# Moving the rotation of the next queries and the query product inside the steps of an attention

## The reference

```
q = (x @ Wq.T).reshape(b, s, 16, 128); k, v likewise with 4 heads
q = q * cos + rotate_half(q) * sin;    k = k * cos + rotate_half(k) * sin
scores = q k^T * 128**-0.5, masked;    attn = softmax(scores)
out = (attn v) reshaped to (b, s, 2048) @ Wo.T
```

## Time and profile before

| | |
|---|---|
| three runs | 840.57, 841.95, 836.37 us |
| the profiled execution: its time | 835.15 us |
| its span | 833.3 us |
| mean granted TensorE clock | 0.936 |
| PE busy | 712.8 us (86%) |
| DVE busy | 627.9 us (75%) |
| ACT busy | 458.0 us (55%) |
| POOL busy | 402.5 us (48%) |

### The profile page before, as it was taken

One profiled execution on the slowest core, in us unless ns is written; L12 is line 12 of the kernel. 1 busy time (PEld: TensorE's weight loads), 2 busy tenths in 40 slices (PEclk: granted clock), 3 DMA queues, 4 the chain that ended last, 5 costly groups with the idle time before them and its releaser, 6 DMA issues. The chain is left out here.

```text
span 833.3 us, 17601 instructions
## 1 busy us (share of the span) xinstructions
PE 712.8 (86%) x5515; PEld 481.6 (58%) x5515; DVE 627.9 (75%) x1436; ACT 458.0 (55%) x1033; POOL 402.5 (48%) x412
## 2 busy tenths in 40 slices
PE   7898969999969999989898699765698498978985
PEld 3555447777637777655555466433586397645652
DVE  5989878778787878699977677544897687676656
ACT  3444568878758888545423266325474476324551
POOL 4544766667667667358636177324004320331440
PEclk9999979999999999999999799966799598998998
DMA  9999995000000000030001233300000010012324
GB/s 375 327 300 185 226 231 2 0 0 0 2 0 1 0 0 0 6 116 1 1 14 58 77 114 110 129 1 1 1 1 2 7 46 2 1 52 84 116 84 164
DMA packets 64945, 59.07 MB, mean 71 GB/s; under 512 B 29106, under 2 KB 59186, under 8 KB 64370
## 3 DMA queue, kind: packets, MB, share of 16 engines
q1 hardware_dynamic: 60706, 47.85, 23.7%
q0 software_dynamic: 3744, 10.26, 3.5%
q10 hardware_dynamic: 432, 0.15, 0.1%
HBM read 27.92 MB, written 30.33 MB: 70 GB/s over the span
## 5 line engine op out<-in xcount | busy, mean ns | idle before, releaser
L1492 PE MATMUL PS<-XT,WA 128*128 128x512 f16 x432 | 100.4, 380 | 0.0
L607 POOL TENSOR_TENSOR ARENA<-ARENA,ST 128x512 f32<-128x512 f32 x64 | 66.6, 1040 | 64.0 <-DVE ST L1278 64.0
L724 ACT ACTIVATE ARENA<-T 128x512 f16<-128x512 f32 (+1 forms) x56 | 35.2, 628 | 109.9 <-DVE T L1156 102.4
L1492 PE MATMUL PS<-WA,ARENA 128*128 128x256 f16 (+2 forms) x960 | 68.6, 212 | 12.9 <-DVE ARENA L1165 11.9
L1492 PEld LDWEIGHTS PS<-WA,ARENA 128*128 128x128 f16 x960 | 56.6, 97 | 29.4 <-DVE ARENA L1165 18.0
L566 POOL DMA_INDIRECT yt_rows<-WA,DIX x46 | 45.4, 987 | 55.4 <-ACT WA L856 43.4
L1492 PEld LDWEIGHTS PS<-XT,WA 128*128 128x128 f16 (+1 forms) x432 | 42.3, 98 | 44.1 <-issue 0.8
L1492 PE MATMUL PS<-KVR,ARENA 128*128 (+1 forms) x384 | 57.9, 279 | 7.9 <-DVE ARENA L1250 4.6
L1258 DVE TENSOR_REDUCE ST<-PS 128x2 f32<-128x512 f32 x64 | 43.9, 686 | 26.1 <-PE PS L1492 25.3
L757 ACT ACTIVATE ARENA<-PS,ST 128x256 f32<-128x256 f32 x128 | 59.3, 470 | 7.0 <-DVE ST L1261 6.8
L1492 PE MATMUL PS<-XT,WC 128*128 128x512 f16 x264 | 60.6, 379 | 2.4 <-DVE T L1149 1.4
(11 more groups left out here) (184 smaller groups left out, 1803.0 us busy)
## 6 DMA issues: line engine op xcount, KB each, us to landing
xs_rows<-ROUT SPq DMA_DIRECT2D x2, 9252.0 KB, 46.1
WA<-xs_rows SPq DMA_DIRECT2D x46, 129.0 KB
WB<-wb_dram SPq DMA_DIRECT2D x1, 4096.0 KB, 21.4
WC<-wc_dram SPq DMA_DIRECT2D x1, 2304.0 KB, 26.5
WA<-wa_dram SPq DMA_DIRECT2D x4, 512.0 KB, 6.8
WA<-wa_dram SPq DMA_DIRECT2D x1, 2048.0 KB, 12.7
WA<-yt_rows SPq DMA_DIRECT2D x4, 512.0 KB, 4.1
WB<-yt_rows SPq DMA_DIRECT2D x4, 512.0 KB, 5.8
```

The costliest lines, as they stand in the source:

```text
L607: pl.tensor_tensor(pr, pr, rs.broadcast_to([P, 2, S]), ALU.mult).then_inc(norm_done, 1)
L724: sc.activation(HH[r, a, 0, :], T3[r, :], ACT.Copy).then_inc(hid_hi, 1)
L1492: ins = te.matmul(dst, left(a), right(b), start=first and n == 0, stop=last and n == 2, skip_group_check=True)
```

## The change

In `step0` of the first attention, each engine's part of a head's rotation and the query product are put at another place of the same instruction stream. POOL's `rope_sine` goes ahead of the normalising in odd steps. ACT's `rope_swapped` goes to the start of odd steps. DVE's `rope_cosine` goes from behind the row maximum of an even step to the end of the odd step before it. PE's query product goes from the end of its step to right behind the scores. No instruction and no wait is added or taken away.

```diff
--- before.py
+++ after.py
@@ -601,12 +601,12 @@
                     rope_add(r + 1, 1)
                 if x == 2 and more:
                     rope_add(r + 2, 0)
+                if x % 2 and more:
+                    rope_sine(r + 2 + x // 2, x // 2)
                 pool.wait_ge(recip_done, st + 1)
                 pr = PR0[:, x % 2, :].rearrange("p (q k) -> p q k", q=2)
                 rs = ST[:, x % 2, 3, :].rearrange("p (q k) -> p q k", k=1)
                 pl.tensor_tensor(pr, pr, rs.broadcast_to([P, 2, S]), ALU.mult).then_inc(norm_done, 1)
-                if x % 2 and more:
-                    rope_sine(r + 2 + x // 2, x // 2)
 
             def attention0(hf, n, th):
                 for i in range(KV0 + 2):
@@ -744,6 +744,8 @@
             def step0(hf, p, x):
                 st, r = NS0 * hf + 4 * p + x, RU * hf + KV0 + 2 * p
                 more, before = not (isinstance(p, int) and p >= P0 - 1), not (isinstance(p, int) and p in (0, P0))
+                if x % 2 and more:
+                    rope_swapped(r + 2 + x // 2, QB, x // 2)
                 if lagged(p, x, 2, P0):
                     act.wait_ge(pt_done, st - 1)
                     after(act, pv_done, st - 3)
@@ -761,9 +763,6 @@
 
                     act.wait_ge(pv_done, st - 2)
                     sc.activation(OT0[:, 1 - x % 2, 0, :], PS[:, OB, 0:S], ACT.Copy, scale=1 / SP).then_inc(ot_hi, 1)
-                if x % 2 and more:
-                    rope_swapped(r + 2 + x // 2, QB, x // 2)
-
                 if x == 0 and before:
                     act.wait_ge(scores, st)
                     rope_high(r + 1, 1, QT0[:, 1, 0, :])
@@ -1260,10 +1259,6 @@
                     dve.wait_ge(max_done, st + 1)
                     v.tensor_scalar(ST[:, x % 2, 1, :], ST[:, x % 2, 0, :], -SC0 / SQ ** 2, None,
                                     ALU.mult).then_inc(shift_done, 1)
-                if x == 0 and before:
-                    rope_cosine(r + 1, QB, 1)
-                if x == 2 and more:
-                    rope_cosine(r + 2, QB, 0)
                 if x == 1 and before:
                     rope_low(r + 1, 1, QT0[:, 1, 1, :], QT0[:, 1, 0, :])
                 if x == 3 and more:
@@ -1280,6 +1275,8 @@
                     dve.wait_ge(ot_hi, st - 2)
                     v.scalar_tensor_tensor(OT0[:, 1 - x % 2, 1, :], PS[:, OB, 0:S], 1 / SP, OT0[:, 1 - x % 2, 0, :],
                                            ALU.mult, ALU.subtract).then_inc(ot_lo, 1)
+                if x % 2 and more:
+                    rope_cosine(r + 2 + x // 2, QB, x // 2)
 
             def attention0(hf, n, th):
                 r = RU * hf
@@ -1686,6 +1683,8 @@
                             te.matmul(PS[:, bank, P:S], IDB[:, :], MASK[:, :], start=False, stop=True,
                                       skip_group_check=True)
                     ins.then_inc(scores, 1)
+                if x in ((1, 2) if isinstance(p, int) and p == 0 else (0, 2)) and not (isinstance(p, int) and p >= P0 - 1):
+                    queries(hf, 2 * p + 2 + x // 2, QB, r + 2 + x // 2, r + 2 + x // 2)
                 if lagged(p, x, 2, P0):
                     pe.wait_ge(norm_done, st - 1)
                     after(pe, pt_lo, st - 3)
@@ -1712,8 +1711,6 @@
                                       lambda s: WB16[:, 2 * pp + xx // 2, s, D:2 * D], False, False)
                     ins.then_inc(proj_done, 1)
 
-                if x in ((1, 2) if isinstance(p, int) and p == 0 else (0, 2)) and not (isinstance(p, int) and p >= P0 - 1):
-                    queries(hf, 2 * p + 2 + x // 2, QB, r + 2 + x // 2, r + 2 + x // 2)
 
             def attention0(hf, n, th):
                 r = RU * hf
```

## The result

The changed kernel takes 887.82 us in the median of four runs (883.76 to 890.63), the kernel before 839.45 (836.37 to 841.95). The ratio is 1.057, with a 95% interval of 1.051 to 1.064. The forecast was 888 us, with a range of 876 to 899.

The account below looks back on a forecast made before the run. PE was taken to bound the pair at 6.66 us; a ring of 8.62 us adds 47.0 over 24 pairs plus 2.6 at the starts, +49.6 us, giving 884.8 or 890.2. The forecast was 888 us, range 876 to 899.

Parts of the forecast that it names:

- What bounds the pair: First attention's loop, before: PE bounds a pair of steps, 6.22 us of work and 0.44 of waits in 6.66.
- The ring: First attention's loop: waits through PE, ACT and DVE close once per pair, summing to 8.62 us, 1.96 more than 6.66.
- the step from the output copy to `rope_high`: On ACT in the even step: 0.40 us from the output copy's start, then `rope_high` for 0.63.
- the transposes to the copy: From the start of PE's transposes to the start of ACT's copy that waits for them: 0.64 us.
- The term for the output's low part: On DVE in the odd step: 0.34 us until the cosine product starts; by the skill's rule 0.42, ring 8.70.
- How often: First attention: 24 pairs at 1.96 us make 47.0, plus 2.6 at the starts of both halves, +49.6 us.
- the one turn at the start of each half: One more ring turn at each half's start, costing 0 to 1.96 us; taken as 1.3, 2.6 for both.
- from the last query product to the last reciprocal of a half: End of each half: the last pair has no query product and stays as it is, 0 us.
- The parts at no cost: POOL's sine product has 3.1 us to spare; DVE's row maximum releases exponentials that wait for ACT's copy anyway: no cost.
- The delay did close into a ring: Rival, no ring: only the even step's transposes come later, 0.8 us in 24 pairs, 19 us, 854; 5%.
- The faster case: Rival: PE never waits ahead of the query product, 0.21 us per pair goes, 5 us, 830 or 834; 2%.
- The clock rival: Rival: PE's waits drop its clock to 1.2 GHz, a pair's PE work is 12.4 us, some 978; 3%.

Follow-up runs that it names:

- e12_cos_early_red: Changed kernel with DVE's cosine product moved behind `rope_low` of the odd step and the row maximum's scaling written as TENSOR_REDUCE; 840.34 us, 0.996 of before.
- e13_T_red: As e12_cos_early_red, with PE's query product moved between the transposes and the value product; 833.97 us, 0.987 of before.
- e1: Changed kernel with only DVE's cosine product moved behind `rope_low` of the odd step, ahead of the reciprocal and the output's low part; 856.17 us, 1.014 of before.
- e3: Kernel before with only PE's query product moved right behind the scores; 896.67 us, 1.059 of before.
- e4: Changed kernel with only POOL's sine product put back behind the normalising; 896.81 us, 1.063 of before.
- e14: Changed kernel with the scaling of the row maximum written as TENSOR_REDUCE; 894.07 us, 1.059 of before.
- e8: Changed kernel with only DVE's cosine product put back behind the row maximum of the next even step; 938.62 us, 1.111 of before.
- e2_query_back: Changed kernel with only PE's query product put back at the end of its step, behind the projection; 862.91 us, 1.023 of before.
- e5_T_scalar: As e13_T_red, but with the scaling in its old form, TENSOR_SCALAR; 855.61 us, 1.013 of before.
- e16_query_back_red: As e2_query_back, with the scaling written as TENSOR_REDUCE; 859.96 us, 1.017 of before.

## Why the prediction was right

**What bounds the pair.** Right: e12_cos_early_red and e13_T_red show that with no ring a pair goes to 6.6 and 6.4 us, PE's own work plus small waits.

**The ring.** Right in mechanism and place. Its sum was forecast at 8.62 us and measured 8.50 and 8.58. The term that was off is the step from the output copy to `rope_high`: I took 0.40 us, the distance to the swapped copies in the earlier trace rows, and it is 0.26 (158.43 to 158.69), in front of 0.67 for `rope_high` in place of its length of 0.63. The others held within 0.02, except for the transposes to the copy, 0.63 and 0.72 for a forecast 0.64. e1 (one edge of the ring out), e3 (a ring of its own from one move), e4 and e14 (not on the ring) and e8 (a longer ring) bear it out.

The term for the output's low part, 0.34 by the row, came out as 0.34 (162.41 to 162.75) and not 0.42. The section of the Trainium skill that the prediction set against it (page "VectorE: DVE Perf Modes", "The DRAIN you can't avoid") also says that a next operation that is not held starts earlier, which the prediction left out.

**How often.** The total of 49.6 us met the 49.7 measured in the attention by luck: three of its parts were off and made up for one another. From one query product to the next, start to start, the trace gives:

| | forecast | measured |
|---|---|---|
| the 24 pairs | +47.0 us | +46.0 us |
| the one turn at the start of each half, both together | +2.6 us | -2.0 us |
| from the last query product to the last reciprocal of a half, both together | 0 | +5.6 us |

The 46.0 hold 1.8 us of one pair of 10.27 us in the first half, where the clock was at its low level; its query product took 2.74 us in place of 1.47:

```profile
127.75 2.74 PE L1489 MATMUL PS<-XT,WB 128*128 128x512 f16 x6 [1.36 <-DVE T L1243]
...
138.02 1.47 PE L1489 MATMUL PS<-XT,WB 128*128 128x512 f16 x6 [1.42 <-DVE T L1243]
```

The turn at a half's start was forecast 1.3 us longer and became shorter, from 5.97 and 6.09 us to 5.17 and 4.94. The end of a half was said to stay and became 2.8 us longer, 18.6 in place of 15.75. The prediction counted query products and passed over their move inside the step: the transposes, the value product and the projection of the step, 1.75 us of PE work by the earlier trace rows, stood ahead of the last query product and now stand behind it. Most of the remaining 1.1 us at an end are longer waits of PE for DVE. At the end of the first half they are 0.81 and 1.14 us for the output's low part (at 231.28 and 235.03); before they were 0.42 for it and 0.55 for `rope_low` (at 207.24 and 209.26).

**The parts at no cost.** POOL's sine product cost nothing that shows: undoing its move made nothing faster (e4). That the cosine product's neighbours on DVE cost nothing held for the changed kernel only because ACT was late for another reason. The same change puts POOL's sum beside DVE's scaling, which took 0.74 us in even steps of the changed kernel where it took 0.17. I had named the POOL instructions as harmless by their readers alone, and not looked at which DVE instructions they run beside.

**The rivals.** The delay did close into a ring. The faster case was far off for this order. It came in e13_T_red, which keeps only the moves on ACT and POOL, has the cosine product and the query product at other places than the change, and the scaling in another form. The clock rival was right in kind and small here: one stretch of 8 us. In e8_cos_back, where PE waited 2.7 us in each pair in place of 1.7 to 1.9, it came again and again. The page "TensorE: Matmul & The Clock Gate" of the Trainium skill, section "A second HAM failure mode: psum-queue depth-cycling", which the prediction cites, is thus borne out in e8_cos_back (clock 0.74 and 0.91) and not in the changed kernel from 138 us to the end of its loop (1.00).

## What to carry to other kernels

Before an instruction is moved ahead of others on its engine, follow its wait round: who frees it, what that one waits for, and whether the chain comes back to what is now queued behind. The sum of that chain is the period, however idle each engine looks; here 8.5 us with no engine over 80% busy in these pairs. When such a move loses, the cure may be a few places elsewhere in the chain: with the instruction that frees the bank moved earlier, three quarters of the loss were gone. The rest took a look at what the moved instructions now run beside; with the scaling in another form the time was that of the kernel before, and with the query product behind the transposes 1.3% under it.

## What the runs showed of the hardware

- A DVE TENSOR_SCALAR of 128x2, SBUF to SBUF, that comes while POOL works on its 128x512 TENSOR_TENSOR doesn't finish before POOL's has: 1.21, 1.14 and 0.74 us in place of 0.17, each end within 0.04 us of POOL's (after, e1_cos_early, e2_query_back, e5_T_scalar). As a TENSOR_REDUCE with the same output it is 0.16 us beside the same POOL instruction (e12_cos_early_red, e14_after_red). The Trainium skill, page "SBUF — State Buffer", section "Who interferes with whom", says that copies and tensor_scalar can run in a mode that takes a port pair shared with GpSimd, which the one that issues first holds for its whole instruction, and that tensor_reduce on trn2 never contends. These times agree; in which mode the scaling ran, no run shows.
- `rope_low`, a DVE TENSOR_TENSOR with both inputs in SBUF, also took longer beside POOL: 1.72 us when it started 0.10 us after POOL's sine product (e16_query_back_red), and 0.69 without. It ended 0.55 us after POOL, not with it.
- In these rows ACT starts an instruction that reads SBUF 0.26 us after the start of the output copy from PSUM (158.43 to 158.69), and one that reads PSUM 0.40 us after it (156.71 to 157.11 in the earlier trace rows).
- In e8_cos_back, where PE stood 2.7 us ahead of each query product, its granted clock fell to the 1.2 GHz level in alternate pairs of most of the loop (0.91 from 180 to 200 us). In the changed kernel it stayed at 1.00, the 2.4 GHz level, from 138 us on through pairs of 8.5 us with 1.7 to 1.9 of standing. In e3_query_only, with the same 1.8 us of standing, it stayed there too except near the start of each half (0.84 and 0.83).
